# The first transfer of x issued as two, one for each half of the partitions

## What is computed

```python
# x: (4, 512, 32, 48) float32, conv_w: (512, 512, 1, 9), conv_b: (512,), prelu_a: scalar
def _L0_conv_ref(feature, conv_w, conv_b, prelu_a):
    Wc = conv_w[:, :, 0, 4]
    def step(prev, x_i):
        y = jnp.einsum('oc,nch->noh', Wc, prev) + conv_b[None, :, None]
        y = jnp.where(y >= 0, y, prelu_a * y)
        cur = y + x_i
        return (cur, cur)
    x = jnp.moveaxis(feature, 3, 0)
    _, fwd_rest = jax.lax.scan(step, x[0], x[1:])
    fl = jnp.concatenate([x[0:1], fwd_rest], axis=0)
    _, bwd_rest = jax.lax.scan(step, fl[-1], fl[:-1], reverse=True)
    out = jnp.concatenate([bwd_rest, fl[-1:]], axis=0)
    return jnp.moveaxis(out, 0, 3)

x = x + _L0_conv_ref(_gn(x), conv_w, conv_b, prelu_a)   # _gn: group norm, 32 groups of 16 channels, eps 1e-5
```

## Time and profile before

| | us |
|---|---|
| median of 3 runs | 376.29 |
| lowest and highest | 376.28 and 376.46 |
| the profiled execution's own time | 376.38 |
| its span, from the first to the last instruction | 374.6 |
| PE busy | 351.7 (94%) |
| DVE busy | 286.0 (76%) |
| ACT busy | 230.0 (61%) |
| POOL busy | 17.3 (5%) |

### The profile page before, as it was taken

How to read it: one execution, slowest core, us unless ns; L and a number is a source line. 1 busy time by engine, 2 the same in 40 slices (tenths; PEclk the granted TensorE clock), 3 DMA queues, 4 the chain that set the end, 5 groups by cost and what they waited for, 6 DMA issues and landing times.

```text
span 374.6 us, 10099 instructions
## 1 busy us (share of the span) xinstructions
PE 351.7 (94%) x3100; PEld 350.6 (94%) x3100; DVE 286.0 (76%) x925; ACT 230.0 (61%) x810; POOL 17.3 (5%) x30
## 2 busy tenths in 40 slices
PE   0279999999999999999999999999999999999996
PEld 0179999999999999999999999999999999999996
DVE  2688899788887887665666878778778787787786
ACT  2886656656556566565565665655656657566564
POOL 2078000000000000000000000000000000000000
PEclk9999999999999999999999999999999999999999
DMA  8998000000000000000000121211212212122122
GB/s 308 429 412 308 2 0 1 0 0 0 1 0 0 1 0 0 0 0 0 0 0 0 59 84 56 84 66 73 84 56 84 82 58 84 61 79 84 56 112 84
DMA packets 10088, 26.30 MB, mean 70 GB/s; under 512 B 1248, under 2 KB 1504, under 8 KB 9440
## 3 DMA queue, kind: packets, MB, share of 16 engines
q1 hardware_dynamic: 10080, 26.22, 18.1%
HBM read 13.63 MB, written 12.58 MB: 70 GB/s over the span
## 4 chain that ended last, share of the span: by engine, by line
PE 91%; DMA 6%; SPq 1%; DVE 1%; ACT 1%; issue 0%; ACTq 0%
PE psum L352 88%; DMA xin<-in_x 6%; PE psum L312 1%; SPq L234 1%; PE psum L302 1%; DVE state L535 0%; DVE state L530 0%; ACT state L382 0%; ACT state L376 0%; PE psum L277 0%; PE psum L273 0%; PE psum L266 0%; ACT above L445 0%; PE psum L295 0%; PE psum L289 0%
## 5 line engine op out<-in xcount | busy, mean ns | idle before, releaser
L352 PE MATMUL psum<-state,w_t 128*128 (+1 forms) x2976 | 332.6, 275 | 0.0
L352 PEld LDWEIGHTS psum<-state,w_t 128*128 128x128 f32 x2976 | 332.5, 192 | 0.0
L445 ACT ACTIVATE above<-psum,params 128x128 f32<-128x128 f32 x376 | 139.7, 372 | 129.6 <-PE psum L352 128.7
L530 DVE TENSOR_TENSOR state<-above,state 128x128 f32 (+1 forms) x376 | 108.4, 288 | 66.1 <-ACT above L445 56.4
L447 ACT ACTIVATE below<-psum,negative 128x128 f32<-128x128 f32 x376 | 139.9, 372 | 0.0
L535 DVE SCALAR_TENSOR_TENSOR state<-below,negative,state 128x128 f32 (+1 forms) x376 | 123.4, 349 | 6.7
L582 DVE TENSOR_TENSOR state<-state,xin (+1 forms) x45 | 30.8, 684 | 0.0
L475 DVE TENSOR_SCALAR state<-xin,mean,rstd 128x320 f32<-128x320 f32 (+2 forms) x72 | 27.9, 435 | 0.0
L457 DVE BATCH_NORM_STATS2 bstat<-xin 128x6 f32<-128x512 f32 x32 | 20.0, 672 | 8.7 <-DMA xin<-in_x 8.7
L266 PE MATMUL psum<-chan,centre 128*128 128x64 f32 (+1 forms) x8 | 2.1, 361 | 18.7 <-DVE chan L471 18.7
L266 PEld LDWEIGHTS psum<-chan,centre 128*128 128x128 f32 x8 | 1.6, 251 | 19.0 <-issue 15.5
(11 more groups left out here) (38 smaller groups left out, 24.6 us busy)
## 6 DMA issues: line engine op xcount, KB each, us to landing
out_y<-state SPq DMA_DIRECT2D x47, 256.0 KB, 2.0
xin<-in_x SPq DMA_DIRECT2D x5, 1536.0 KB, 12.8
xin<-in_x SPq DMA_DIRECT2D x3, 768.0 KB, 21.8
xin<-in_x SPq DMA_DIRECT2D x7, 256.0 KB, 18.1
w_t<-in_w SPq DMA_DIRECT2D x4, 256.0 KB, 10.6
xin<-in_x SPq DMA_DIRECT2D x1, 512.0 KB, 24.1
out_y<-state SPq DMA_DIRECT2D x1, 192.0 KB, 1.9
out_y<-state SPq DMA_DIRECT2D x1, 64.0 KB, 1.6
```

What stands on the lines that cost most here:

```text
L352: mm = nc.tensor.matmul(psum[:, 4 * par + o, 0:COLS], w_t[:, k, o * P:(o + 1) * P], xs[k], start=k == 0, stop=k == 3)
L445: nc.scalar.activation(above[:, par, o, :], z, ACT.Relu, bias=params[:, o:o + 1], scale=1.0).then_inc(above_done, 1)
L530: nc.vector.tensor_tensor(sts[o], above[:, par, o, :], sts[o], ALU.add).then_inc(part_done, 1)
```

## The change

The first transfer (block 0, which carries block 1 with it) is issued as two: partitions 0 to 63 of both blocks, then partitions 64 to 127 of both. Both raise the same semaphore, each by 16, so the readers of blocks 0 and 1 wait for 32. Every other transfer stays as it is, one behind the two.

```diff
 P = 128
+HALF = P // 2
...
                 for i, size in enumerate(pieces(b)):
-                    sp.dma_start(xin[:, b // N, b % N:n1, w0:w0 + size, :],
-                                 x[b // N, :, b % N:n1, w0:w0 + size, :]).then_inc(x_loaded[b][i], 16)
+                    for p0 in range(0, P, HALF if b == 0 else P):
+                        p1 = p0 + (HALF if b == 0 else P)
+                        sp.dma_start(xin[p0:p1, b // N, b % N:n1, w0:w0 + size, :],
+                                     x[b // N, p0:p1, b % N:n1, w0:w0 + size, :]).then_inc(x_loaded[b][i], 16)
                     w0 += size
...
             def unit_mean(nth):
                 rec, part, size, loaded = act_unit(nth)
-                act.wait_ge(loaded, 16)
+                act.wait_ge(loaded, 32 if nth < 2 else 16)
...
             def unit_stats(b, i):
                 w0, w1, piece, _ = units(b)[i]
-                dve.wait_ge(x_loaded[b][piece], 16)
+                dve.wait_ge(x_loaded[b][piece], 32 if b < 2 else 16)
```

## The result

| | before | after |
|---|---|---|
| median of 5 runs, us | 376.30 | 379.95 |
| lowest and highest | 376.28 and 376.57 | 379.76 and 379.98 |
| span of the profiled execution | 374.6 | 378.2 |

The change makes the kernel 3.65 us slower: 1.0092 of the time before, 95% interval 1.0081 to 1.0103. The range of the prediction (376.2 to 380.1) holds it, 379.4 was forecast, and the likeliest case's own range was 378.8 to 380.1.

The account below looks back on a forecast made before the run. The stream of x, with full DMA engines and no slack, was taken to set the time before an unchanged recurrence; 3.3 - 0.1 + 0.02, less 0.1 for overlap, made +3.1 on 376.29: 379.4 us, range 376.2 to 380.1.

Parts of the forecast that it names:

- the likeliest case: First transfer: full halving of the rate, the two halves one behind the other; 379.4 us, chance 0.62.
- What bounds: Loading stage: a later stream of x delays every later step equally, and the recurrence keeps its length.
- The rate of the two halves: First transfer: 64 partitions move at half of 430 GB/s; +3.66 less 0.34 hidden by the slow start, taken as +3.3.
- The first bytes: Stream start: a half has fewer rows to set up, so data begins earlier; -0.1, bounds -0.19 and 0.
- One more end of a transfer: End of the added transfer: one more small packet on each engine; +0.02, bounds 0 and +0.05.
- A little overlap: First transfer: engines starting apart let a little of one half run beside the other; -0.1.
- SP's queue: SP's issues: later loads are issued up to 0.47 us later but stay ahead of the data; cost 0.
- the waits for 32: Readers of the first transfer wait for both halves; later pieces land as much later, so nothing is added.
- the clock: PE: its idle matmuls follow the landings and move with them, so no change of its clock is counted.
- The rival of overlap: First transfer: engines out of step share lanes, so the halves overlap; +0.8 to +2.5, middle 378.0 us, chance 0.16.
- The rival on the other side: First transfer: each engine's own pace is the bound, rate stays 430; -0.19 to +0.05, 376.2 us, chance 0.18.
- The rival of a better start: Stream start: smaller first transfers bring engines in together, recovering up to 0.91 us, down to 375.4 us; chance 0.04.

Follow-up runs that it names:

- the cut by image: Against the changed kernel, the first transfer is two by image, each over all 128 partitions, with the same wait for 32: 376.63 us, +0.12 above the kernel before.
- quarters: Against the changed kernel, the first transfer is four of 32 partitions each, with waits for 64: 379.60 us, +3.15 above the kernel before.
- the second place: Against the changed kernel, blocks 2 and 3 are cut in partition halves, first transfer whole: 380.35 us; with both pairs cut, 383.61 us.
- The three-part kernel: Against the changed kernel, the first transfer is three, partitions 0 to 31, 32 to 95, 96 to 127: 380.11 us, run again 378.11 us.

## Why the prediction was right, point by point

- **What bounds.** That the stream of x has no slack in the direction of later, and that the recurrence keeps its length, held to 0.1 us: first reader +3.56, last sums +3.57, span +3.6.
- **The rate of the two halves** (+3.3 of between 0 and 3.66). Right in kind: in the windows the halves move at 197 to 233 GB/s with a share near 1, and the cut by image, with the same count and the same waits, costs 0.12. In size it is +3.15 where the first bytes are not late (quarters), or 3.65 less the late start of about 0.35, 3.3. That the slow start hides 0.34 of it is not shown: in the second place, where there is no slow start, the cut costs 3.84 alone but 3.51 behind the first, on either side of the full 3.66.
- **The first bytes** (-0.1 of between -0.19 and 0). The step that was wrong, in its sign. A first transfer of 64 partitions is issued in 0.56 and not 0.38, and its bytes begin after 2.00, where in the kernel before they began ahead of 2.00. Every kernel with 64 partitions in the first place shows it (0.56 to 0.63), those with 128 or 32 do not (0.38, 0.39). I had let half of the issue's time go by the number of rows; that the bounds excluded a loss had no row behind it.
- **One more end of a transfer** (+0.02 of 0 to 0.05). Not to be told from nothing: +0.12 for the cut by image, within its interval.
- **A little overlap** (-0.1). Not decided: 3.3 for the change leaves no room for it, the quarters' 3.15 does, and their interval is some 0.5 us wide to either side. Without it, the whole miss of 0.55 is accounted for: 0.45 is the start (+0.35 where I had -0.1), and 0.1 is this.
- **SP's queue, the waits for 32, the clock.** As said, no cost: the idle time before the last pieces is 0.39 against 0.41, and the granted clock is 1.00 in every window shown.

The Trainium skill's page "SBUF — State Buffer" spoke against the change in its sections "Door 1: The DMA port swizzle" and "Can I just issue two DMAs to hit both halves?". The runs agree with the first: parts of 32 partitions move about as fast as parts of 64 (218 and 233 GB/s from 3 to 7), and 32 to 95, which by its map reach all the ports, at full rate (418). They agree with the second in that the two serialize (landings after 6.2 and 10.1 us); its 6% is not to be seen (379.95 both ways).

The rival of overlap would have shown the first rows on DVE between 8 and 9.7 and a rate between 215 and 430 GB/s; they came at 10.80, with windows of 197 to 233. The rival on the other side, the engine's own pace as the bound, would have shown 430 GB/s in halves and first rows at 7.1 to 7.3. The rival of a better start had the sign of the start wrong, as I had.

## What to carry to other kernels

In a stretch that the DMA stream bounds, cut a load along its free dimensions and keep all 128 partitions in every part: two parts by image cost 0.12 us, two by partitions 3.65. Before cutting by partitions, ask which partitions are in a part, and not how many: here 0 to 63, 64 to 127 and quarters of 32 ran at half the rate, 32 to 95 at all of it. A DMA share near 1 says only that packets are under way, so read it beside the GB/s. A delay at the head of a stream without holes is paid in full at its end, here 27 us later.

## What the runs showed that was not expected

As the first of the program, a transfer of 64 partitions takes SP longer to issue than one of 128 with the same 768 KB (0.56 to 0.63 against 0.38), and one of 32 does not (0.39); this delays the first bytes by about 0.35 us. It does not go by the number of partitions alone: right behind an issue of 64, one of 32 took 0.56 and 0.58 too, where behind one of 32 it took 0.41. Why is open. And two halves issued at once from two queues went one behind the other, ACT's first. The three-part kernel has executions of 378 and of 380 to 381 side by side, for which no profile was caught either.
